# Holding seven half-units of batch 1 instead of six, and re-spacing the reloads of batch 0, in a two-pass kernel bound by its transfers

## The chip, the cores and the metric

The kernel runs on one core of a Trainium2 chip. The metric is the device time of one execution in microseconds. The kernel before took 1709.55 us (median of three runs, 1707.28 to 1709.72).

## The reference, cut to what matters

`x` has the shape (2, 512, 256, 256), f32: 2 batches, 512 channels, 268 MB. The output has the same shape.

```python
xn = group_norm(x)                      # 32 groups of 16 channels, mean and variance per (b, group)
xl1 = relu(batch_norm(depthwise(xn, w1)))   # w1: 256 x 1, contracts the rows    -> (b, c, 256)
xl2 = relu(batch_norm(depthwise(xn, w2)))   # w2: 1 x 256, contracts the columns -> (b, c, 256)
dot = sum(xl1 * xl2, axis=-1)           # (b, c); the einsum's result is read as c x b and reshaped
num = softmax((dot.reshape(b, c) @ lw1.T + lb1) @ lw2.T + lb2, axis=1)
out = x + xn * num[:, :, None, None]    # = x * scale(b, group, channel) + shift(b, group, channel)
```

The einsum `bck,bck->cb` followed by `reshape(b, c)` mixes the batches: row 0 of the softmax needs the dot products of both batches over channels 0 to 255, row 1 those over channels 256 to 511. So the scales of batch 0 are known when half of the channels of both batches have been read, those of batch 1 only when everything has.

## The kernel before

The work is cut into half-units (u, b): u from 0 to 63 is one half of the rows of a group of 16 channels (group g = u // 2), b is the batch. A half-unit is 128 partitions x 4096 f32 = 2048 KB. There are 128 of them; on the chip there are eleven places for one: ten buffers of `xs` (0 to 9) and `filters` (number 10, called FILTERS).

The pass reads every half-unit once for its statistics. Per half-unit ACT squares it (L805), PE convolves it with w1 (L576, in the last three groups L591, one batch at a time), and DVE multiplies the rows with w2 and sums them (16 row instructions at L1002, or one product and one reduction over the whole half-unit at L1028 and L1031, or sums of products that POOL made). Scaling and storing comes later, and what has left its buffer by then has to be loaded again:

- Batch 0, units 0 to 31: the first four scaled are still in their buffers (KEPT = 4), the other 28 are loaded again ("reloads" 0 to 27, `load_again`, L331) during the second half of the pass. ACT scales each (L878) and stores it (L883) in `rework(r)`.
- Batch 0, units 32 to 63: scaled in their buffers as soon as the group's statistics are there (`scale_first` on DVE, L1104; `store_first` on ACT).
- Batch 1: all 64 are scaled after the pass. The last HELD ones are still in their buffers, the others are loaded again (L378), scaled by DVE (L1174) and stored by ACT in the order LAST_ORDER, round the eleven places of `last_slot`. This last stretch is called the tail.

All orders are written out by hand. SP issues every load in one fixed order and waits before each until the buffer is free, so a load that waits holds up all loads behind it. ACT issues nearly all stores, in its program order. In the second half of the pass a step is a pair (g, b): SP issues the two loads of it, then the reload whose number REWORK_AT assigns to step 2g + b. ACT does that reload's scaling in the same step. `rework_slot(r)` gives a reload its buffer (2, 3 and 8 in turn for most), `slot_of(u, b)` gives a half-unit of the pass its buffer: batch 1 takes 6 and 7 in turn, except those held to the end.

`softmax(1)` at the end of the pass (L1166) is a chain through all engines: the last row sums on DVE, `normalise(15)`, `rectify(15)` and `exponential(1)` on ACT (L863, L869, L874), the logits on PE, the coefficients on DVE. Only then may the first half-unit of batch 1 be scaled and stored.

Line numbers are those of the kernel before; everything below the edit is five to seven lines further down in the changed one.

Of the kernel before, what the change touches and what calls it, by code (L numbers as in the profile page):

```python
# [11 lines left out]
UNITS = 2 * G  # L12
S = 11
SCRATCH, FILTERS = 9, 10
# [17 lines left out]
FIRST = UNITS // 2  # L32
# [1 line left out]
FQ = Q // 2  # L34
RING3 = 27
KEPT = 4
HELD = 6
REWORK = FIRST - KEPT
PROD_SLOT = SCRATCH
PROD_GROUPS = range(FG + 2, G - 4)  # L40
CHUNKS = 2
CHUNK_ROWS = JH // CHUNKS
REWORK_AT = list(range(FIRST + 1, UNITS - 6)) + [UNITS - 5, UNITS - 3]
ACT_SCALES = G - 3
SPLIT = G - 3
LAST_ORDER = list(range(UNITS - HELD, UNITS)) + list(range(UNITS - HELD))
# [17 lines left out]
def slot_of(u, b):  # L64
    if u < RING3:
        return u % 3 + 4 * b
    if u < FIRST:
        return u % 4 + 4 * b
    if b == 0:
        return (4, 5, 0, 1)[u % 4]  # L70
    return {UNITS - 6: 9, UNITS - 5: 2, UNITS - 2: 4, UNITS - 1: 5}.get(u, 6 + u % 2)


def rework_slot(r):
    if r < 2:
        return (8, PROD_SLOT)[r]
    if r < REWORK - 4:
        return (2, 3, 8)[(r - 2) % 3]
    return (3, 8, 3, 8)[r - REWORK + 4]


def last_slot(i):
    return (9, 2, 6, 7, 4, 5, 3, 8, 0, 1, FILTERS)[i % S]


LOADS = [[] for _ in range(S)]
# [26 lines left out]
def conv_preact(nc, x, w1, w2, g1, b1, g2, b2, w2_rows, lw1, lb1, lw2, lb2, out):  # L113
# [9 lines left out]
    with ExitStack() as ctx:  # L123
# [172 lines left out]
        @block.sync  # L296
        def _(sp):
            def free_of_statistics(u, b):
                sp.wait_ge(rows_done, rows_before(u, b) + SETS)
                sp.wait_ge(squared, position(u, b) + 1)  # L300
                if u < FIRST:
                    sp.wait_ge(multiplied, position(u, b) + 1)
                sp.wait_ge(pe_read_x, filters_before(u, b))

            def load(u, b):
                s = slot_of(u, b)
                n = LOADS[s].index(("x", u, b))
                if n == 0 and s in (3, 7):
                    sp.wait_ge(mixed_copied, CT)
                    sp.wait_ge(bias_copied, 1)  # L310
                elif n:
                    before = LOADS[s][n - 1]
                    if before in STORES[s]:
                        sp.wait_ge(x_stored[s], written(s, before))
                        if s == PROD_SLOT:
                            sp.wait_ge(rows_done, rows_before(2 * PROD_GROUPS[-1] + 1, 0) + SETS)
                    else:
                        free_of_statistics(before[1], before[2])
                sp.dma_start(xs[:, s, :], x_v[u // 2, :, b, part_of(u)]).then_inc(x_loaded[s], 16)

            def load_again(r):
                s = rework_slot(r)
                n = LOADS[s].index(("re", r))
                if s == SCRATCH and n == 0:
                    sp.wait_ge(y2_done, FIRST)
                if n:
                    before = LOADS[s][n - 1]
                    if before[0] == "x":
                        before = ("x", FIRST - KEPT + s, 0)
                    sp.wait_ge(x_stored[s], written(s, before))  # L330
                sp.dma_start(xs[:, s, :], x_v[r // 2, :, 0, part_of(r)]).then_inc(x_loaded[s], 16)  # L331

            sp.dma_start(w2_c[:], w2_rows.rearrange("(t p) w -> p t w", p=P)).then_inc(w2c_loaded, 16)
            load(0, 0)
            sp.dma_start(w1_sb[:], w1).then_inc(w1_loaded, 16)
            load(0, 1)
            load(1, 0)
            load(1, 1)
            sp.dma_start(w2_sb, w2).then_inc(w2_loaded, 16)
            for i, v in enumerate((g1, b1, g2, b2)):  # L340
                sp.dma_start(affine_in[:, i], v.unsqueeze(0).to_broadcast([GB, CG, G])).then_inc(small_loaded, 16)
            sp.dma_start(lb1_sb[:], lb1).then_inc(small_loaded, 16)
            sp.dma_start(bias[:], lb2).then_inc(small_loaded, 16)
            load(2, 0)
            load(2, 1)
            sp.wait_ge(taps_summed, 1)
            sp.dma_start(lw1_sb.rearrange("p (t b) o k -> p t b (o k)", b=B),
                         lw1.rearrange("(t p b) o -> p t b o", p=P, b=B)).then_inc(lw1_loaded, 16)
            sp.dma_start(lw2_sb, lw2.rearrange("(o p) c -> p o c", p=P)).then_inc(lw2_loaded, 16)
            for u in range(3, FIRST):  # L350
                for b in range(B):
                    load(u, b)

            load_again(0)
            for u, b in SEQUENCE[2 * FIRST:2 * FIRST + 4]:
                load(u, b)
            load_again(1)
            for i in range(0, KEPT, 2):
                u = FIRST - KEPT + i
                sp.wait_ge(scaled_kept[0], i // 2 + 1)  # L360
                sp.dma_start(out_v[u // 2, :, 0, part_of(u)], xs[:, slot_of(u, 0), :]
                             ).then_inc(x_stored[slot_of(u, 0)], 16)
            for g in range(FG + 1, G):
                for b in range(B):
                    for hf in range(2):
                        load(2 * g + hf, b)
                    if 2 * g + b in REWORK_AT:
                        load_again(REWORK_AT.index(2 * g + b) + 1)

            for i in range(HELD, UNITS):  # L370
                s, u = last_slot(i), LAST_ORDER[i]
                if i >= S:
                    sp.wait_ge(x_stored[s], written(s, ("last", i - S)))
                elif s == FILTERS:
                    sp.wait_ge(pe_read_x, filters_before(UNITS - 1, 1))
                else:
                    sp.wait_ge(x_stored[s], written(s, LOADS[s][LOADS[s].index(("last", i)) - 1]))
                sp.dma_start(buffer(s), x_v[u // 2, :, 1, part_of(u)]).then_inc(x_loaded[s], 16)  # L378
            for s in range(S):
                sp.wait_ge(x_stored[s], 16 * len(STORES[s]))  # L380
# [418 lines left out]
        def _(act):  # L799
# [52 lines left out]
            def normalise(q):  # L852
                r = rstd_a[:, q, QG * B:] if q < FQ else rstd_b[:, QG * (q + 1) - 1 - FG, B:2 * B]
                act.wait_ge(off_ready, q + 1)
                act.wait_ge(folded, QG * (q + 1))
                act.wait_ge(y2_turned, q + 1)
                if q:
                    act.wait_ge(dots_ready, 2 * q)
                if q == FQ:
                    act.wait_ge(prob_turned, 1)  # L860
                for i, (to, y) in enumerate(((z, ps_y1), (ps_y2, ps_y2))):
                    for b in range(B):
                        nc.scalar.activation(to[:, b * W:(b + 1) * W], y[:, b * W:(b + 1) * W], ACT.Identity,  # L863
                                             scale=r[:, b:b + 1], bias=off[:, i, b:b + 1]).then_inc(z_done, 1)

            def rectify(q):
                act.wait_ge(affine_ready, q + 1)
                for i, y in enumerate((z, ps_y2)):
                    nc.scalar.activation(y[:], y[:], ACT.Relu, scale=bn_a[:, i:i + 1],  # L869
                                         bias=bn_b[:, i:i + 1]).then_inc(relu_done, 1)  # L870
# [14 lines left out]
            def rework(r):  # L885
                s = rework_slot(r)
                act.wait_ge(x_loaded[s], landed(s, ("re", r)))
                scaled_by_act(s, r // 2, reworked, r + 1)
                store(r, 0, s)
# [35 lines left out]
            for i in range(1, KEPT, 2):  # L925
                u = FIRST - KEPT + i
# [4 lines left out]
            for u, b in SEQUENCE[2 * FIRST:]:  # L931
                if u % 2 == 0 and b == 0 and u // 2 in PROD_GROUPS:
                    copy_w2_late(u // 2)
                square(u, b)
                if u % 2:
                    if u // 2 >= SPLIT:
                        copy_part(u // 2, b)
                    elif b:
                        copy_parts(u // 2)
                        store_first(u // 2)  # L940
                    if u - 1 + b in REWORK_AT:
                        rework(REWORK_AT.index(u - 1 + b) + 1)
                elif b and u // 2 >= SPLIT:
                    store_first(u // 2)
                for q in range(FQ, Q - 1):
                    if position(u, b) == stage(q, 23):
                        normalise(q)
                    if position(u, b) == stage(q, 27):
                        rectify(q)
            normalise(Q - 1)  # L950
            rectify(Q - 1)
            exponential(1)
# [254 lines left out]
```

## Time and profile before

| | |
|---|---|
| median of 3 runs | 1709.55 us |
| the profiled execution | 1705.58 us, its span 1703.8 us |
| busy | DVE 1004.7 us (59%), ACT 665.1 (39%), POOL 508.9 (30%), PE 485.6 (28%) |
| DMA | 723.80 MB at a mean of 425 GB/s |
| first store of batch 1 after the pass | issued at 1128.04 us |

The profile was taken in one execution. "DMA share" is the mean busy share of the core's 16 DMA engines; a share of 1.00 or 1.01 means that they had work all the time. The DMA queue q1 carries the loads, which SP issues, and q10 the stores, which ACT issues. A transfer's time to landing counts from its issue, so it includes the time that it stood behind others in its queue. Microseconds in the rows count from the start of the span.

### The profile page before, as it was taken

The page shows a single profiled execution, that of the slowest core. Times are in us where ns is not written, and L with a number is a line of the kernel's source. Part 1 is how long each engine was busy: PE and PEld are TensorE (multiplying, and loading weights), DVE is VectorE, ACT ScalarE, POOL GpSimd, SP SyncE. Part 2 cuts the span into 40 slices and gives each one's busy share as a digit, 9 for nine tenths or more (in the row PEclk, how much of TensorE's full clock was granted, in tenths as well). Part 3 has the DMA queues.
Part 4 walks back from the last instruction along what each step waited for, and adds up shares of the span by engine and source line. Part 5 has one row for each costly group of instructions (what it writes and reads, how often), then busy time and mean ns, then how long its engine had stood idle before and what let it go on. Part 6 is the DMA issues. An engine that isn't in the chain of part 4 may idle for free.

```text
span 1703.8 us, 14430 instructions
## 1 busy us (share of the span) xinstructions
PE 485.6 (28%) x3416; PEld 169.7 (10%) x3416; DVE 1004.7 (59%) x2672; ACT 665.1 (39%) x517; POOL 508.9 (30%) x489
## 2 busy tenths in 40 slices
PE   3588766660223321223333243430000000000000
PEld 1123212120001100001001021210000000000000
DVE  5899999967757576776666786772222222222220
ACT  4688887856435455544445546600000000000000
POOL 7678787820315444443254000000000000000000
PEclk8799878885666665666566566665555555555555
DMA  9999999989999999999999999999999999999999
GB/s 393 426 425 427 427 428 426 428 338 419 432 428 431 431 430 431 430 432 430 432 430 430 431 428 430 430 385 431 431 432 431 432 431 431 432 431 432 431 431 408
DMA packets 52126, 723.80 MB, mean 425 GB/s; under 512 B 6241, under 2 KB 6753, under 8 KB 8034
## 3 DMA queue, kind: packets, MB, share of 16 engines
q1 hardware_dynamic: 33922, 458.84, 63.4%
q10 hardware_dynamic: 18144, 264.25, 36.3%
q8 instruction: 27, 0.44, 0.1%
q14 instruction: 33, 0.27, 0.0%
HBM read 454.63 MB, written 268.44 MB: 424 GB/s over the span
## 4 chain that ended last, share of the span: by engine, by line
DMA 39%; another core or an unknown queue 26%; DVE 8%; PE 3%; issue 2%; ACT 2%; SPq 1%; DVEq 1%; POOL 0%; ACTq 0%; POOLq 0%
DMA xs<-in_x 28%; DMA out<-xs 11%; DVE xs L1104 3%; PE ps_part L576 2%; DVE xs L1028 1%; DVE mul_junk L1002 1%; DVE y2s L1031 1%; SPq L378 1%; ACT xs L878 1%; PE ps_part L710 1%; ACT sq_junk L805 1%; DVEq L1002 0%; DVE xs L1002 0%; POOL rstd_b L468 0%
## 5 line engine op out<-in xcount | busy, mean ns | idle before, releaser
L805 ACT ACTIVATE sq_junk<-xs 128x4096 fp8e5<-128x4096 f32 x128 | 463.1, 3618 | 203.9 <-DMA xs<-in_x 198.6
L576 PE MATMUL ps_part<-xs,filters 128*32 128x512 f32 x1856 | 290.8, 781 | 525.3 <-DMA xs<-in_x 516.2
L1104 DVE TENSOR_SCALAR xs<-xs,scale,shift 128x4096 f32<-128x4096 f32 x90 | 222.8, 2496 | 353.9 <-DMA xs<-in_x 353.3
L1002 DVE SCALAR_TENSOR_TENSOR xs<-xs,ps_w 128x256 f32 (+1 forms) x832 | 294.5, 416 | 28.6 <-DMA xs<-in_x 18.4
L534 POOL TENSOR_TENSOR xs<-xs,w_late 128x2048 f32<-128x2048 f32 x40 | 179.6, 4526 | 102.6 <-ACT w_late L819 102.6
L878 ACT ACTIVATE xs<-xs,shift,scale 128x4096 f32<-128x4096 f32 x33 | 125.3, 3798 | 157.3 <-DVE xs L1104 135.5
L576 PEld LDWEIGHTS ps_part<-xs,filters 128*32 128x32 f32 x1856 | 79.3, 138 | 718.3 <-issue 718.3
L1028 DVE TENSOR_TENSOR xs<-xs,ps_w 128x4096 f32<-128x4096 f32 x26 | 114.7, 4413 | 52.8 <-PE ps_part L576 46.6
L468 POOL TENSOR_TENSOR rstd_b<-var,minus_half 128x2 f32<-128x2 f32 (+1 forms) x23 | 15.2, 661 | 417.2 <-DVE var L1054 417.2
L1022 DVE TENSOR_REDUCE y2s<-xs 128x8 f32<-128x2048 f32 x40 | 91.4, 2286 | 77.1 <-POOL xs L534 77.1
L439 POOL TENSOR_TENSOR xs<-xs 128x768 f32<-128x768 f32 x64 | 116.7, 1827 | 58.0 <-DMA xs<-in_x 55.0
L1002 DVE SCALAR_TENSOR_TENSOR mul_junk<-xs,ps_w 128x256 uint8<-128x256 f32 x288 | 104.1, 417 | 30.5 <-DVE mul_junk L1002 15.9
L1031 DVE TENSOR_REDUCE y2s<-xs 128x16 f32<-128x4096 f32 x26 | 114.9, 4420 | 2.7
L1002 DVE DVE_READ_ACCUMULATOR xs<-xs,ps_w (+1 forms) x832 | 68.3, 82 | 0.0
L445 POOL TENSOR_TENSOR xs<-xs 128x384 f32<-128x384 f32 x64 | 63.1, 1009 | 0.0
L591 PE MATMUL ps_part<-xs,filters 128*32 128x256 f32 x384 | 38.6, 566 | 52.8 <-DMA xs<-in_x 52.8
L449 POOL TENSOR_TENSOR xs<-xs 128x192 f32<-128x192 f32 x64 | 36.8, 600 | 0.0
L409 POOL TENSOR_TENSOR filters<-own,filters 128x512 f32<-128x512 f32 x32 | 33.9, 1059 | 6.9 <-PE ps_part L591 6.7
L604 PE MATMUL ps_y<-y_part,fold 128*32 128x512 f32 x64 | 31.0, 615 | 4.5 <-ACT y_part L833 4.4
L826 ACT ACTIVATE y_part<-ps_part 128x256 f32<-128x256 f32 x58 | 21.6, 382 | 26.4 <-PE ps_part L576 17.8
L672 PE MATMUL ps_l<-xs 128*128 128x512 f32 x64 | 29.6, 605 | 0.0
L1104 DVE TENSOR_SCALAR filters<-filters,scale,shift 128x4096 f32<-128x4096 f32 x5 | 12.1, 2410 | 29.2 <-DMA filters<-in_x 29.2
(116 smaller groups left out, 458.4 us busy)
## 6 DMA issues: line engine op xcount, KB each, us to landing
xs<-in_x SPq DMA_DIRECT2D x209, 2048.0 KB, 24.0
out<-xs ACTq DMA_DIRECT2D x121, 2048.0 KB, 27.6
filters<-in_x SPq DMA_DIRECT2D x5, 2048.0 KB, 18.0
out<-filters ACTq DMA_DIRECT2D x5, 2048.0 KB, 86.2
xs<-in_lw SPq DMA_DIRECT2D x2, 2048.0 KB, 16.3
out<-xs SPq DMA_DIRECT2D x2, 2048.0 KB, 12.1
filters<-in_w_rows SPq DMA_DIRECT2D x1, 512.0 KB, 3.8
filters<-in_w SPq DMA_DIRECT2D x1, 512.0 KB, 8.9
```

The source lines that it names most:

```text
L439: nc.gpsimd.tensor_tensor(prod[:, b], xs[:, s, DVE_ROWS * W:].rearrange("p (r w) -> p r w", w=W), w2_copy[:, g % 2].unsqueeze(1).to_broadc ...
L445: nc.gpsimd.tensor_tensor(prod[:, b, :, 0:128], prod[:, b, :, 0:128], prod[:, b, :, 128:256], ALU.add).then_inc(added, 1)
L534: nc.gpsimd.tensor_tensor(chunk(c), x_rows[:, c * CHUNK_ROWS:(c + 1) * CHUNK_ROWS], w2_late[:].unsqueeze(1).to_broadcast([P, CHUNK_ROWS, W ...
L576: last = nc.tensor.matmul(ps_part[g % 2][32 * a:32 * a + 32, :], taps[:, g % 2, hf * JH + j, :], xs[:, s[0]:s[1] + 1:s[1] - s[0], j * W:(j ...
L591: last = nc.tensor.matmul(ps_part[b][32 * a:32 * a + 32, 0:W], taps[:, g % 2, hf * JH + j, :], xs[:, s, j * W:(j + 1) * W], start=(hf == 0 ...
L805: nc.scalar.activation(sq_junk[:], xs[:, s, :], ACT.Square, accum_out=sq_sum[:, u % 2, u // 2, b:b + 1], saturate=False).then_inc(squared, 1)
L878: nc.scalar.activation(xs[:, s, :], xs[:, s, :], ACT.Identity, scale=scale[:, 0, g:g + 1], bias=shift[:, 0, g:g + 1]).then_inc(done, 1)
L1002: return nc.vector.scalar_tensor_tensor(out=out, in0=x_row, scalar=1.0, in1=ps_w2[g % 2][:, 0:W], op0=ALU.mult, op1=ALU.mult, accum_out=total)
L1022: nc.vector.tensor_reduce(sums[:, c * CHUNK_ROWS:(c + 1) * CHUNK_ROWS], chunk(c), AX.X, ALU.add).then_inc(rows_done, SETS // CHUNKS)
L1028: nc.vector.tensor_tensor(x_rows, x_rows, ps_w2[g % 2][:, 0:W].unsqueeze(1).to_broadcast([P, JH, W]), ALU.mult).then_inc(products_done, 1)
L1031: nc.vector.tensor_reduce(sums, x_rows, AX.X, ALU.add).then_inc(rows_done, SETS)
L1104: return nc.vector.tensor_scalar(buffer(s), buffer(s), scale[:, b, g:g + 1], shift[:, b, g:g + 1], ALU.mult, ALU.add)
```

## The change

One more half-unit of batch 1, (57, 1), stays in its buffer at the end of the pass (HELD = 7, in buffer 8), so the tail has 57 loads in place of 58. The reloads of batch 0 move: three steps in the middle of the second half of the pass (38, 43 and 48) issue two reloads each; behind step 54 only step 57 has one; the last reload (27) is issued behind all loads of the pass, and ACT scales and stores it behind the last half-unit and ahead of `normalise(15)`. The tail goes round its places in another order. Since (57, 1) is now held, DVE treats it with 16 row instructions, as it did the six.

```diff
@@ -34,13 +34,14 @@
 FQ = Q // 2
 RING3 = 27
 KEPT = 4
-HELD = 6
+HELD = 7
 REWORK = FIRST - KEPT
 PROD_SLOT = SCRATCH
 PROD_GROUPS = range(FG + 2, G - 4)
 CHUNKS = 2
 CHUNK_ROWS = JH // CHUNKS
-REWORK_AT = list(range(FIRST + 1, UNITS - 6)) + [UNITS - 5, UNITS - 3]
+TWICE = (FIRST + 6, FIRST + 11, FIRST + 16)
+REWORK_AT = sorted([*range(FIRST + 1, UNITS - 9), *TWICE, UNITS - 7])
 ACT_SCALES = G - 3
 SPLIT = G - 3
 LAST_ORDER = list(range(UNITS - HELD, UNITS)) + list(range(UNITS - HELD))
@@ -68,19 +69,23 @@
         return u % 4 + 4 * b
     if b == 0:
         return (4, 5, 0, 1)[u % 4]
-    return {UNITS - 6: 9, UNITS - 5: 2, UNITS - 2: 4, UNITS - 1: 5}.get(u, 6 + u % 2)
+    return {UNITS - 7: 8, UNITS - 6: 9, UNITS - 5: 2, UNITS - 2: 4, UNITS - 1: 5}.get(u, 6 + u % 2)
 
 
 def rework_slot(r):
     if r < 2:
         return (8, PROD_SLOT)[r]
-    if r < REWORK - 4:
+    if r < REWORK - 2:
         return (2, 3, 8)[(r - 2) % 3]
-    return (3, 8, 3, 8)[r - REWORK + 4]
+    return 3
+
+
+def reworks_at(step):
+    return [r for r, at in enumerate(REWORK_AT, 1) if at == step]
 
 
 def last_slot(i):
-    return (9, 2, 6, 7, 4, 5, 3, 8, 0, 1, FILTERS)[i % S]
+    return (8, 9, 2, 6, 7, 4, 5, FILTERS, 0, 1, 3)[i % S]
 
 
 LOADS = [[] for _ in range(S)]
@@ -364,8 +369,9 @@
                 for b in range(B):
                     for hf in range(2):
                         load(2 * g + hf, b)
-                    if 2 * g + b in REWORK_AT:
-                        load_again(REWORK_AT.index(2 * g + b) + 1)
+                    for r in reworks_at(2 * g + b):
+                        load_again(r)
+            load_again(REWORK - 1)
 
             for i in range(HELD, UNITS):
                 s, u = last_slot(i), LAST_ORDER[i]
@@ -938,8 +944,8 @@
                     elif b:
                         copy_parts(u // 2)
                         store_first(u // 2)
-                    if u - 1 + b in REWORK_AT:
-                        rework(REWORK_AT.index(u - 1 + b) + 1)
+                    for r in reworks_at(u - 1 + b):
+                        rework(r)
                 elif b and u // 2 >= SPLIT:
                     store_first(u // 2)
                 for q in range(FQ, Q - 1):
@@ -947,6 +953,7 @@
                         normalise(q)
                     if position(u, b) == stage(q, 27):
                         rectify(q)
+            rework(REWORK - 1)
             normalise(Q - 1)
             rectify(Q - 1)
             exponential(1)
```

On SP, around step 43 (both rows of loads of group 21 batch 1, its reload, then group 22), the kernel before has this order; x_stored2 means that the transfer waits until what stood in buffer 2 has been stored:

```order
L319 DMA xs<-in_x 128x4096 [waits pe_read_x,squared,rows_done] x2
L331 DMA xs<-in_x 128x4096 [waits x_stored2]
L319 DMA xs<-in_x 128x4096 [waits x_stored4]
L319 DMA xs<-in_x 128x4096 [waits x_stored5]
L331 DMA xs<-in_x 128x4096 [waits x_stored3]
L319 DMA xs<-in_x 128x4096 [waits pe_read_x,squared,rows_done] x2
L331 DMA xs<-in_x 128x4096 [waits x_stored8]
```

The same place in the changed kernel:

```order
L324 DMA xs<-in_x 128x4096 [waits pe_read_x,squared,rows_done] x2
L336 DMA xs<-in_x 128x4096 [waits x_stored3]
L336 DMA xs<-in_x 128x4096 [waits x_stored8]
L324 DMA xs<-in_x 128x4096 [waits x_stored4]
L324 DMA xs<-in_x 128x4096 [waits x_stored5]
L336 DMA xs<-in_x 128x4096 [waits x_stored2]
L324 DMA xs<-in_x 128x4096 [waits pe_read_x,squared,rows_done] x2
```

Two reloads (12 and 13, buffers 3 and 8) now stand ahead of the loads of group 22; the second waits for the store of a reload two steps back, where every reload before waited for one three steps back.

On SP, from (54, 0) to (59, 1), before. The two rows with x2 are (54, 1), (55, 1) and (56, 1), (57, 1):

```order
L319 DMA xs<-in_x 128x4096 [waits x_stored1]
L331 DMA xs<-in_x 128x4096 [waits x_stored8]
L319 DMA xs<-in_x 128x4096 [waits pe_read_x,squared,rows_done] x2
L331 DMA xs<-in_x 128x4096 [waits x_stored2]
L319 DMA xs<-in_x 128x4096 [waits x_stored4]
L319 DMA xs<-in_x 128x4096 [waits x_stored5]
L331 DMA xs<-in_x 128x4096 [waits x_stored3]
L319 DMA xs<-in_x 128x4096 [waits pe_read_x,squared,rows_done] x2
L331 DMA xs<-in_x 128x4096 [waits x_stored8]
L319 DMA xs<-in_x 128x4096 [waits x_stored0]
L319 DMA xs<-in_x 128x4096 [waits x_stored1]
```

The same half-units in the changed kernel:

```order
L324 DMA xs<-in_x 128x4096 [waits x_stored1]
L336 DMA xs<-in_x 128x4096 [waits x_stored8]
L324 DMA xs<-in_x 128x4096 [waits pe_read_x,squared,rows_done] x2
L324 DMA xs<-in_x 128x4096 [waits x_stored4]
L324 DMA xs<-in_x 128x4096 [waits x_stored5]
L324 DMA xs<-in_x 128x4096 [waits pe_read_x,squared,rows_done]
L324 DMA xs<-in_x 128x4096 [waits x_stored8]
L336 DMA xs<-in_x 128x4096 [waits x_stored3]
L324 DMA xs<-in_x 128x4096 [waits x_stored0]
L324 DMA xs<-in_x 128x4096 [waits x_stored1]
```

The reloads before are 22, 23, 24 and 25; now they are 25 and 26. The load of (57, 1) goes to buffer 8 and waits for the store of reload 25.

On SP, from (60, 1) to the first loads of the tail, before:

```order
L319 DMA xs<-in_x 128x4096 [waits pe_read_x,squared,rows_done] x2
L331 DMA xs<-in_x 128x4096 [waits x_stored8]
L319 DMA xs<-in_x 128x4096 [waits x_stored0]
L319 DMA xs<-in_x 128x4096 [waits x_stored1]
L319 DMA xs<-in_x 128x4096 [waits x_stored4]
L319 DMA xs<-in_x 128x4096 [waits x_stored5]
L378 DMA xs<-in_x 128x4096 [waits x_stored3]
L378 DMA xs<-in_x 128x4096 [waits x_stored8]
L378 DMA xs<-in_x 128x4096 [waits x_stored0]
L378 DMA xs<-in_x 128x4096 [waits x_stored1]
L378 DMA filters<-in_x 128x4096 [waits pe_read_x]
L378 DMA xs<-in_x 128x4096 [waits x_stored9]
```

The same place in the changed kernel:

```order
L324 DMA xs<-in_x 128x4096 [waits pe_read_x,squared,rows_done] x2
L324 DMA xs<-in_x 128x4096 [waits x_stored0]
L324 DMA xs<-in_x 128x4096 [waits x_stored1]
L324 DMA xs<-in_x 128x4096 [waits x_stored4]
L324 DMA xs<-in_x 128x4096 [waits x_stored5]
L336 DMA xs<-in_x 128x4096 [waits x_stored3]
L384 DMA filters<-in_x 128x4096 [waits pe_read_x]
L384 DMA xs<-in_x 128x4096 [waits x_stored0]
L384 DMA xs<-in_x 128x4096 [waits x_stored1]
L384 DMA xs<-in_x 128x4096 [waits x_stored3]
L384 DMA xs<-in_x 128x4096 [waits x_stored8]
```

Reload 27 moved from ahead of (62, 0) to behind (63, 1). Before, five loads of the tail came ahead of the first that waits for a store of batch 1 (x_stored9); now four do, and `filters` is the first of them in place of the last.

## Rows read from the trace of the kernel before

**Rows 1.** The profile's page: span, DMA busy tenths and GB/s in 40 slices.
```profile
span 1703.8 us, 14430 instructions
...
DMA  9999999989999999999999999999999999999999
GB/s 393 426 425 427 427 428 426 428 338 419 432 428 431 431 430 431 430 432 430 432 430 430 431 428 430 430 385 431 431 432 431 432 431 431 432 431 432 431 431 408
```
**Rows 2.** Stretches: us, PE, PEld, DVE, ACT, POOL busy, clock, DMA share, GB/s.
```profile
600.00:800.00 200.00, 55.95 (x390) 17.73 (x390) 139.60 (x75) 101.09 (x67) 83.02 (x38) 0.64 1.01 431
...
950.00:1104.00 154.00, 66.15 (x566) 28.75 (x566) 115.23 (x471) 89.45 (x58) 8.12 (x19) 0.62 1.01 430
```
**Rows 3.** The same view, the end of the pass and the tail.
```profile
1104.00:1136.00 32.00, 15.63 (x120) 7.92 (x120) 20.05 (x55) 5.21 (x12) 3.28 (x10) 0.67 0.93 374
1112.00:1124.00 12.00, 9.14 (x22) 3.60 (x22) 3.24 (x10) 4.02 (x8) 1.88 (x7) 0.74 0.79 315
1136.00:1680.00 544.00, 0.00 (x0) 0.00 (x0) 143.06 (x60) 0.00 (x0) 0.00 (x0) 0.50 1.01 431
```
**Rows 4.** The page: DMA issues, KB each, median us to landing.
```profile
xs<-in_x SPq DMA_DIRECT2D x209, 2048.0 KB, 24.0
out<-xs ACTq DMA_DIRECT2D x121, 2048.0 KB, 27.6
filters<-in_x SPq DMA_DIRECT2D x5, 2048.0 KB, 18.0
out<-filters ACTq DMA_DIRECT2D x5, 2048.0 KB, 86.2
...
out<-xs SPq DMA_DIRECT2D x2, 2048.0 KB, 12.1
```
**Rows 5.** Timeline of SP's queue at the end of the pass: start us, us.
```profile
1120.51 0.43 SPq L378 DMA_DIRECT2D filters<-in_x  x1
```
**Rows 6.** That transfer by its line: us from issue to landing.
```profile
DMA to landing us min/median/max: 13.4/13.4/13.4
```
**Rows 7.** Timeline of SP's queue around (57, 1).
```profile
954.83 19.75 SPq L319 DMA_DIRECT2D xs<-in_x  x4
984.08 0.33 SPq L331 DMA_DIRECT2D xs<-in_x  x1
```
**Rows 8.** Timeline of PE: the convolution of (57, 1); brackets: idle before, released by.
```profile
975.57 4.96 PE L576 MATMUL ps_part<-xs,filters 128*32 128x512 f32 x32 [3.38 <-DMA xs<-in_x]
```
**Rows 9.** Timeline of ACT at the end of the pass.
```profile
1101.01 3.62 ACT L805 ACTIVATE sq_junk<-xs 128x4096 fp8e5<-128x4096 f32 x1 [0.47 <-ACT xs L878]
...
1111.89 0.56 ACT L863 ACTIVATE z<-ps_y,off,rstd_b 128x256 f32<-128x256 f32 x1 [6.81 <-PE ps_y L616]
```
**Rows 10.** Timeline of ACT's queue: the stores of the tail begin.
```profile
1128.04 21.24 ACTq L883 DMA_DIRECT2D out<-xs  x10
```
**Rows 11.** Waits of DVE, 1035 to 1095 us: us in total, times, longest.
```profile
DVE mul_junk L1002 <- DMA xs<-in_x: 13.8, 4, 6.9
```
**Rows 12.** Timeline of DVE: (57, 1), then (62, 0) and what follows it.
```profile
990.12 4.41 DVE L1028 TENSOR_TENSOR xs<-xs,ps_w 128x4096 f32<-128x4096 f32 x1
994.63 4.42 DVE L1031 TENSOR_REDUCE y2s<-xs 128x16 f32<-128x4096 f32 x1
...
1075.49 0.42 DVE L1002 SCALAR_TENSOR_TENSOR mul_junk<-xs,ps_w 128x256 uint8<-128x256 f32 x1 [3.90 <-DMA xs<-in_x]
...
1081.97 0.15 DVE L1048 TENSOR_SCALAR nmean<-ps_m 128x1 f32<-128x1 f32 x1
```
**Rows 13.** The page: ACT scales a reload; busy us, mean ns | idle before.
```profile
L878 ACT ACTIVATE xs<-xs,shift,scale 128x4096 f32<-128x4096 f32 x33 | 125.3, 3798 | 157.3 <-DVE xs L1104 135.5
```
**Rows 14.** Timeline of SP's queue: the reloads of steps 45 and 46.
```profile
657.34 0.47 SPq L331 DMA_DIRECT2D xs<-in_x  x1
...
678.82 0.33 SPq L331 DMA_DIRECT2D xs<-in_x  x1
```
**Rows 15.** Loads of line L319 issued from 600 to 700 us.
```profile
DMA to landing us min/median/max: 23.8/32.0/36.5
```

## The prediction, made before the changed kernel had run

> **What bounds the kernel now.** I read the page's slices of DMA first, then stretches of the same counters, and only then single engines. The DMA engines are busy at nine tenths or more in all slices but one, and they move 426 to 432 GB/s in most of them [rows 1]. Two slices of the 40 stand out: 338 in slice 9 and 385 in slice 27 [rows 1]. The change touches only the second. In the second half of the pass and in the tail the DMA share is 1.00 or 1.01 at 430 to 431 GB/s [rows 2, 3], while DVE, the busiest engine, has 140 us of 200 [rows 2]. So the time is the bytes, at 430 GB/s, and the places where the transfers run dry. One transfer of 2048 KB (2.097 MB) costs 2.097 / 430 = 4.88 us. There are 342 of them (209 + 5 loads, 121 + 5 + 2 stores [rows 4]), which is 1669 us of the span of 1704.
>
> The dry place is the end of the pass. From 1104 to 1136 us the rate is 374 in place of 430: 32 x (1 - 374/430) = 4.2 us are lost [rows 3]; 3.2 of them lie in 1112 to 1124, at 315 GB/s [rows 3]. There the chain of `softmax(1)` runs, no half-unit of batch 1 may be stored before 1128.04 [rows 10], and the reloads that could fill the time wait in SP's queue: the one into `filters` was issued at 1120.51 [rows 5] and landed 13.4 us later [rows 6], behind two that waited for the stores of (62, 0) and (63, 0), though PE had long left `filters`.
>
> **The sum is made against the profiled execution**, 1705.6 us (span 1703.8). The median of the runs is 1709.55, 4.0 us more; I take the difference worked out here to the median.
>
> **One reload less.** The tail has 57 loads in place of 58: -4.9 us. Nothing covers a transfer where the share is 1.01 for 544 us [rows 3], so this is on the path in full.
>
> **The dry place.** To be moved between the last load of the pass and the first store of batch 1 were five tail loads, the store of reload 27 and two stores; now four tail loads, reload 27 with its load and store, and the two stores: one transfer more of cover. `filters` comes first and waits only for PE, so it can flow while the stores of (62, 0) and (63, 0) are under way. How much of the 4.2 us comes back depends on when compute releases the first store of batch 1 against when the DMA has moved all that stands ahead of it. The second time: before, the `filters` load landed at 1133.9; from 1128.0 it shared the engines with stores, so half of these 5.9 us, 2.9, was its own. 1128.0 + 2.9 - 4.2 (dry) - 4.9 (the reload less) = 1121.8 us. Every us that the first store comes after 1121.8 is lost.
>
> **When compute is ready.** The anchor is (57, 1): PE starts to convolve it at 975.57, released by its load [rows 8]. From there to the first store of batch 1 are 1128.04 - 975.57 = 152.5 us. In these DVE waited four times for loads of the pass, 13.8 us in all [rows 11]; with three reloads fewer between (57, 1) and (63, 1) these waits go. DVE also works less: (57, 1) took 4.4 + 4.4 us as product and reduction, 16 row instructions take 1081.97 - 1075.49 = 6.5 [rows 12]: -2.3. So the floor is 152.5 - 13.8 - 2.3 = 136.4 us behind the landing of (57, 1). Any faster pass ends on DVE, no longer on the loads.
>
> That landing comes later, since reloads have moved ahead of it. Counted in transfers: before, reloads 0 to 24 were loaded ahead of (57, 1), and the stores of 0 to 23 had landed (the fourth of SP's loads from 954.83, which needs store 23, leaves at 974.3; reload 26, which needs store 24, at 984.08 [rows 7]). Now 0 to 25 are loaded ahead of it and the stores of 0 to 25 have landed, because its buffer waits for store 25. That is one load and two stores: 3 x 4.88 = 14.6 us. The load is issued earlier than before, so a part of the stores of (54, 0) and (55, 0) may fall behind it: 0 to 9.8 us off. I take half a transfer: +12.2, so 987.8. The first store then comes at 987.8 + 136.4 = 1124.2, and the loss is 1124.2 - 1121.8 = 2.4 us in place of 4.2: -1.8. The bounds: landing 4.9 us later gives 1116.9 and no loss, -4.2; 14.6 later gives 1126.6, a loss of 4.8, +0.6.
>
> A sentence of the Trainium skill speaks against this term: DMA: Bandwidth & Descriptors, "Anatomy of one DMA", gives each transfer a fixed cost of about 2.0 us (fitted for transfers that GpSimd issues), which shows wherever nothing else is under way; the three tail loads that wait for a store each would show it again, so by that page nothing of the 4.2 us comes back and the sum would be the 4.9 of the reload alone. No row here shows the cost by itself. The mechanism by rows: each of these loads is issued only when a store has landed, and 3.2 us were lost with two such loads [rows 3, 5]; now `filters` and reload 27 lie beside them. It is the first rival below.
>
> **Reload 27 ahead of normalise(15) on ACT.** ACT gets its last square at 1101.01, which ends with the copy behind it by 1105.1, and `normalise(15)` starts at 1111.89, released by PE [rows 9]. Scaling a reload takes 3.8 us [rows 13], its issue 0.3: 1109.2, 2.7 us before it is needed. If the reload lands over 2.7 us after ACT is free, the softmax chain and the first store slip by the rest. It follows (63, 1) at once in its queue, 4.9 to 9.8 us behind it (alone, or taking turns with stores), and (63, 1) now comes earlier against DVE. I take 0; the bound is +4.1 (9.8 - 3.0 for the square - 2.7).
>
> **The double steps.** The second reload of a double step waits for a store two steps back. At the same point before, SP passed a reload at 657.34, and the store from two steps back had landed at 678.82 [rows 14]: SP, and with it the loads of the next group, would stand for 21.5 us. In its queue lie then loads issued 23.8 to 36.5 us ahead of their landing [rows 15], one more than before, and the stores. So the DMA does not run dry: 0. Engines wait longer for half-units, which costs nothing while the share is 1.01. If another 9.8 us of waiting for the next reload's store came on top, 31.3 against 23.8 + 4.9 would leave 2.6 us dry, three times: +8.
>
> **Sum:** -4.9 - 1.8 + 0 + 0 = -6.7 us, -0.39%: 1698.9 in the profiled execution, 1702.8 on the median. Its own range, from the bounds of the landing, is -9.1 to -4.3: 1700.4 to 1705.3.
>
> **Rivals.**
> 1. Only the reload is saved; the dry place keeps its 4.2 us since the loads at its end still depend on stores, or ACT's reload delays the chain. -4.9: 1704.7. For it: the loads into buffers 0, 1 and 3 all wait for late stores. Against: one transfer more in the stretch.
> 2. Nothing: the double steps run dry. 1709.55 - 6.7 + 8 = 1710.9, or half of it, 1707. For it: SP's block of 21.5 us is as long as the shortest queue of 23.8. Against: the share of 1.01 through stretches in which SP waits as it is [rows 2]; a deep queue.
> 3. Slower: (57, 1) comes so late that the rest of the pass is bound by DVE. If all three advanced reloads with loads and stores fall ahead of it (6 x 4.88 = 29.3), it lands at 1004.9, the first store of batch 1 is issued at 1141.3, 19.5 us behind 1121.8, and the sum is -4.9 - 4.2 + 19.5 = +10.4: 1719.9. It decides from a loss of 9.1 us on, that is from a landing 18.9 us later than before, four transfers against my three. For it: DVE, once behind, has no slack in 136 us. Against: two of the six transfers come behind (57, 1) by the order itself.
>
> **How the numbers follow.** The forecast 0.50, rival 1 0.22, rival 2 0.17, rival 3 0.11. A measurement of this kernel tells a change from about 0.2% on, 3.4 us; so faster by more is 0.50 + 0.22 = 0.72, within it 0.17, slower 0.11. The predicted time is 1702.8. The range that leaves two in ten out is 1699.5 (the low bound of the forecast and a little for the spread of the runs) to 1709.5 (rival 1 and half of rival 2).
>
> **What would show it.** Right: 341 transfers; DMA share 1.01 in 430 to 1100 us as before; PE's convolution of (57, 1) at 980 to 990; DVE without waits for DMA from (60, 0) on; over 400 GB/s in the 12 us ahead of a first store of batch 1 at 1117 to 1127; ACT's reload 27 done before PE releases `normalise(15)`. Wrong: slices below 425 GB/s between 450 and 950 us (rival 2); that convolution behind 994 and a wide dry stretch ahead of the first store (rival 3); the same 4 us dry and a first store near 1128 (rival 1).

## The result: 0.3% slower, where 0.4% faster was forecast

The changed kernel takes 1712.65 us (median of 9 runs, 1710.7 to 1715.8), the kernel before, beside it, 1708.35 (9 runs). The ratio is 1.0031, 95% interval 1.0022 to 1.0040: 4 to 5 us slower (3.8 to 6.8 by the interval). The forecast was 1702.8, its range 1699.5 to 1709.5. The profiled execution of the changed kernel took 1712.33 us, its span 1710.6, 6.8 us more than before [rows 1].

### The profile after

The page of the changed kernel has the reload less (213 loads against 214), and slices 23 to 27 where the rate falls, where before only slice 27 did [rows 1, 4]:

```profile
span 1710.6 us, 14489 instructions
...
GB/s 394 425 427 427 427 427 426 428 354 417 433 429 432 431 429 432 430 429 432 429 432 431 414 416 395 348 415 427 429 428 431 431 430 433 430 431 433 430 431 402
...
xs<-in_x SPq DMA_DIRECT2D x207, 2048.0 KB, 22.2
...
filters<-in_x SPq DMA_DIRECT2D x6, 2048.0 KB, 18.2
```

Stretches of the changed kernel, with the columns of [rows 2]:

```profile
430.00:950.00 520.00, 137.72 (x946) 44.46 (x950) 332.41 (x175) 256.64 (x167) 204.22 (x91) 0.63 1.01 431
950.00:1050.00 100.00, 45.00 (x386) 18.51 (x382) 84.53 (x251) 47.16 (x37) 9.15 (x14) 0.68 1.00 412
1050.00:1110.00 60.00, 28.36 (x266) 13.73 (x258) 51.00 (x260) 35.49 (x25) 4.41 (x13) 0.73 0.88 354
1110.00:1140.00 30.00, 16.22 (x120) 8.06 (x120) 17.36 (x57) 9.90 (x13) 3.26 (x10) 0.61 1.00 418
1140.00:1680.00 540.00, 0.00 (x0) 0.00 (x0) 146.59 (x62) 0.00 (x0) 0.00 (x0) 0.50 1.01 430
```

The same in the kernel before, for the three in the middle:

```profile
950.00:1050.00 100.00, 39.00 (x344) 16.48 (x344) 74.28 (x267) 53.28 (x35) 5.92 (x13) 0.59 1.01 430
1050.00:1110.00 60.00, 31.48 (x274) 14.85 (x270) 46.09 (x237) 37.24 (x27) 2.20 (x6) 0.67 1.01 430
1110.00:1140.00 30.00, 11.29 (x88) 5.34 (x80) 18.91 (x27) 4.13 (x8) 3.28 (x10) 0.67 0.92 368
```

Against 430 GB/s, before lost 30 x 62/430 = 4.3 us, all in the last stretch. The changed kernel loses 100 x 18/430 = 4.2, 60 x 76/430 = 10.6 and 30 x 12/430 = 0.8, together 15.6. The dry place was cured as forecast (368 to 418), and a larger one opened inside the pass. 15.6 - 4.3 - 4.9 (the reload) = +6.4, of the 6.8 measured between the two spans. That this comes so near is partly luck: in e11, a second profile of the same kernel, the same three stretches lose 12.4 us, and the span is 0.6 us longer. What holds in both is the first store of batch 1: it is 7.6 us later than before (1135.63 against 1128.04), and from it to the end pass 575.0 us, 575.8 before; 7.6 - 0.8 = 6.8. Up to 950 us, through all three double steps, the rate is 431 as before.

What opened it is seen on DVE. Timelines of the end of (55, 1) and the start of (56, 1), before:

```profile
947.81 4.42 DVE L1031 TENSOR_REDUCE y2s<-xs 128x16 f32<-128x4096 f32 x1
...
972.31 4.42 DVE L1028 TENSOR_TENSOR xs<-xs,ps_w 128x4096 f32<-128x4096 f32 x1 [6.35 <-PE ps_part L576]
```

and in the changed kernel:

```profile
977.56 4.42 DVE L1038 TENSOR_REDUCE y2s<-xs 128x16 f32<-128x4096 f32 x1
...
995.63 4.42 DVE L1035 TENSOR_TENSOR xs<-xs,ps_w 128x4096 f32<-128x4096 f32 x1
```

DVE ends (55, 1) at 982.0 in place of 952.2, 29.8 us later: about the six transfers (29.3) of the three reloads moved ahead. Before, after the row sums of (56, 0) and (57, 0), it waited 6.35 us for (56, 1); now it waits for nothing there. PE's timeline of the changed kernel shows when (55, 1) and (57, 1) had come. Before, their rows started at 926.04 and 975.57 [rows 8]; (55, 1) came 29.9 us later, but (57, 1) only 13.2 us:

```profile
955.90 5.23 PE L582 MATMUL ps_part<-xs,filters 128*32 128x512 f32 x32 [4.74 <-DMA xs<-in_x]
...
988.77 5.34 PE L582 MATMUL ps_part<-xs,filters 128*32 128x512 f32 x32 [4.12 <-DMA xs<-in_x]
```

The waits of DVE from 952 to 1136 us in the changed kernel hold no wait for a load at all, where before there were 13.8 us of them [rows 11]; the longest are within the row sums themselves and for POOL:

```profile
DVE mul_junk L1009 <- DVE mul_junk L1009: 14.6, 53, 0.6
DVE scale L1117 <- POOL nmr_b L475: 6.2, 5, 2.3
```

The end of the pass on ACT, changed kernel: store of (63, 0), square and copy of (63, 1), reload 27, normalise, first store of batch 1:

```profile
1107.58 0.34 ACTq L889 DMA_DIRECT2D out<-xs  x1
1108.02 3.62 ACT L811 ACTIVATE sq_junk<-xs 128x4096 fp8e5<-128x4096 f32 x1 [0.47 <-ACT xs L884]
...
1111.99 3.79 ACT L884 ACTIVATE xs<-xs,shift,scale 128x4096 f32<-128x4096 f32 x1
1115.81 0.34 ACTq L889 DMA_DIRECT2D out<-xs  x1
1118.90 1.02 ACT L869 ACTIVATE z<-ps_y,off,rstd_b 128x256 f32<-128x256 f32 x2 [3.12 <-PE ps_y L622]
...
1135.63 2.66 ACTq L889 DMA_DIRECT2D out<-xs  x2
```

Reload 27 is scaled and its store issued 2.7 us before `normalise(15)` starts, and that start still waits for PE: reload 27 did not delay the chain. The first store of batch 1 is issued at 1135.63, 7.6 us later than before [rows 10].

### The profile page after: what moved, and what is told of

It reads as the page before. It is cut to its first block, busy times and chain, and to the rows that moved or that the text cites. A ratio compares the mean times of both kernels' runs of the same rounds, so it can differ in the third digit from the quotient of the medians.

```text
span 1710.6 us, 14489 instructions
## 1 busy us (share of the span) xinstructions
PE 486.4 (28%) x3416; PEld 172.8 (10%) x3416; DVE 1000.8 (59%) x2702; ACT 664.3 (39%) x517; POOL 508.4 (30%) x489
## 4 chain that ended last, share of the span: by engine, by line
DMA 35%; another core or an unknown queue 25%; DVE 10%; issue 5%; PE 3%; ACT 2%; DVEq 2%; SPq 1%; POOL 0%; ACTq 0%; POOLq 0%
DMA xs<-in_x 22%; DMA out<-xs 13%; DVE mul_junk L1009 3%; DVE xs L1111 3%; ACT xs L884 2%; DVE xs L1035 1%; PE ps_part L582 1%; DVEq L1009 1%; SPq L384 1%; DVE y2s L1038 1%; PE ps_part L716 1%; ACT sq_junk L811 1%; DVE xs L1009 0%; DVEq L1040 0%
## 5 line engine op out<-in xcount | busy, mean ns | idle before, releaser
L1035 DVE TENSOR_TENSOR xs<-xs,ps_w 128x4096 f32<-128x4096 f32 x25 | 110.3, 4413 | 71.5 <-PE ps_part L582 65.4
L1009 DVE SCALAR_TENSOR_TENSOR mul_junk<-xs,ps_w 128x256 uint8<-128x256 f32 x304 | 109.8, 417 | 18.9 <-DVE mul_junk L1009 18.2
L1038 DVE TENSOR_REDUCE y2s<-xs 128x16 f32<-128x4096 f32 x25 | 110.5, 4420 | 2.6
L832 ACT ACTIVATE y_part<-ps_part 128x256 f32<-128x256 f32 x58 | 21.6, 381 | 25.7 <-PE ps_part L582 15.6
```

The lines of the kernel that those rows point to most:

```text
L1009: return nc.vector.scalar_tensor_tensor(out=out, in0=x_row, scalar=1.0, in1=ps_w2[g % 2][:, 0:W], op0=ALU.mult, op1=ALU.mult, accum_out=total)
L1035: nc.vector.tensor_tensor(x_rows, x_rows, ps_w2[g % 2][:, 0:W].unsqueeze(1).to_broadcast([P, JH, W]), ALU.mult).then_inc(products_done, 1)
L1038: nc.vector.tensor_reduce(sums, x_rows, AX.X, ALU.add).then_inc(rows_done, SETS)
```

## The experiments

All ratios are to the kernel before on the same chip, with 95% intervals. The runs were made on several chips, so kernels are compared by their ratios, and medians are set side by side only where a chip is shared or the gap is large. "First store" is the issue of the first store of batch 1 in the one profiled execution of each run. The code excerpts show the lines that matter and leave out the rest of the edit. Theory A: the reloads taken out of steps 55 to 61 had covered DVE's work there. The rivals stand in the expectations.

**e1: reload 27 behind the pass, alone** (against the kernel before)

```diff
-REWORK_AT = list(range(FIRST + 1, UNITS - 6)) + [UNITS - 5, UNITS - 3]
+REWORK_AT = list(range(FIRST + 1, UNITS - 6)) + [UNITS - 5]
-    return (9, 2, 6, 7, 4, 5, 3, 8, 0, 1, FILTERS)[i % S]
+    return (9, 2, 6, 7, 4, 5, 3, FILTERS, 0, 1, 8)[i % S]
```

Not shown: the load of reload 27 behind the pass, into buffer 8, and its scaling ahead of `normalise(15)`, as in the change.

> The kernel before with one part of the change alone: reload 27 is issued behind (63, 1), and ACT scales and stores it ahead of normalise(15); six half-units held, the other reloads where they were. Theory A (the change lost its time because the reloads taken out of steps 55 to 61 had covered the time that DVE needs there; DVE was 14 us late for the first store of batch 1): here DVE is not late at (55, 1), its four waits for loads (13.8 us) go, the first store of batch 1 comes near 1114 to 1118 in place of 1128, and the 4.2 us of the dry place go: 1704 to 1706 against 1708.4. Theory B (reload 27 behind the pass is itself what costs, on ACT ahead of the softmax chain or as a dependent tail load): no faster, or 1 to 4 us slower, with the first store of batch 1 at 1128 or later.

1706.01 us, ratio 0.9990 (0.9981 to 0.9999); first store at 1121.79. Behind the pass, reload 27 does no harm: the first store comes 6 us earlier. But that is 4 us later than A's 1114 to 1118, the time only touches the upper end of A's range, and the gain is 2 us where A expected 4.2, because 1050 to 1110 now runs at 410 GB/s (2.8 us lost). So a thin place opens there even where only reload 27 is taken out of the last groups.

**e2 and e12: the reloads moved ahead, alone** (against the changed kernel; e12 is the same kernel again)

```diff
-HELD = 7
+HELD = 6
-REWORK_AT = sorted([*range(FIRST + 1, UNITS - 9), *TWICE, UNITS - 7])
+REWORK_AT = sorted([*range(FIRST + 1, UNITS - 9), *TWICE, UNITS - 7, UNITS - 3])
```

Not shown: the buffers and the order of the tail go back to those of the kernel before, and reload 27 (step 61) is loaded and scaled inside the pass.

> The kernel before with the reloads moved ahead alone: double steps 38, 43, 48, then only steps 57 and 61; six held, the old buffers and the old tail order. Theory A: DVE ends (55, 1) near 982 in place of 952, the first store of batch 1 comes near 1135 to 1138, DMA is short of work from 1050 to 1110, and the kernel is 5 to 8 us slower than before, 1714 to 1716. Theory B (holding a seventh half-unit, the tail's new order or reload 27 costs): within 1 us of before. Theory C (the double steps cost by themselves, SP standing in front of the second reload): slower too, but with the loss between 480 and 800 us, below 425 GB/s there.

> The kernel of e2 (the reloads moved ahead alone, reload 27 at step 61, six held) beside the changed kernel. In the profiled execution of e2 (1714.4 us) the first store of batch 1 came at 1139.7; its median was 4 us below that execution. Theory A: 1713 to 1717 and slower than the changed kernel. If it stays below the changed kernel, holding the seventh half-unit and moving reload 27 behind the pass together cost 2 us and save nothing in this schedule: what they take from the last groups is lost again on DVE.

e2: 1710.51, ratio 1.0022 (1.0011 to 1.0033), first store at 1139.72 in an execution 3.9 us above the median. e12: 1710.71, 1.0022 (1.0013 to 1.0032), first store at 1136.10. The move alone makes the kernel about 4 us slower, where 5 to 8 were expected, so theory B is out. The rate is 431 in 600 to 950 us in both, so theory C is out.

**e11: the changed kernel again, beside e12**

> The changed kernel itself, on the chip and beside the runs of e12. Theory A puts it at 1712 to 1713 again, and below e12 by the reload less, 3 to 5 us, if both lose the same time at the end of the pass. So far their medians (1712.65 and 1710.51, on other chips) say the opposite.

1712.87, ratio 1.0023 (1.0014 to 1.0031); first store at 1135.81. So the changed kernel is not faster than e12 with its 342 transfers; the intervals overlap. Both start the tail at the same time, and have the same tail before them: 64 stores and 53 loads (57 less the four, 58 less the five that come ahead of it). From the first store to the end of the span pass 1711.2 - 1135.8 = 575.4 and 1709.0 - 1136.1 = 572.9 us; 117 transfers at 4.88 are 571. The two kernels differ by one transfer ahead of the first store, and that store is issued at the same time. So by this count the reload that was saved had lain in time that is now dry. This part is argued from the count; e12's 2.5 us less behind the first store are not explained. Stretches of e12, then two of e11:

```profile
950.00:1050.00 100.00, 43.40 (x386) 17.95 (x382) 87.84 (x221) 47.45 (x37) 7.27 (x14) 0.65 1.00 421
1050.00:1110.00 60.00, 29.20 (x266) 13.78 (x258) 50.96 (x259) 39.46 (x26) 4.41 (x13) 0.73 0.99 408
1110.00:1140.00 30.00, 17.01 (x120) 8.07 (x120) 16.67 (x57) 5.89 (x12) 3.27 (x10) 0.61 0.86 361
...
950.00:1050.00 100.00, 46.52 (x389) 18.63 (x382) 84.86 (x252) 47.40 (x37) 9.31 (x14) 0.67 1.01 429
1050.00:1110.00 60.00, 28.09 (x266) 13.29 (x258) 50.90 (x259) 35.49 (x25) 4.40 (x13) 0.70 0.86 344
```

In e11 950 to 1050 us loses 0.2 us, where the first profile of this kernel lost 4.2; 1050 to 1110 loses 12.0 against 10.6. Only the second place belongs to the change in both.

**e4 and e5: a quarter of DVE's row sums left out in units 56 to 63**, in the changed kernel (e4) and in the kernel before (e5)

```diff
-                    for j in range(SET):
+                    for j in range(SET if u < UNITS - 8 else SET - 1):
```

> The changed kernel with a quarter of DVE's row instructions left out in the 15 half-units of units 56 to 63 that are summed row by row (12 of 16 rows each, the row sums of the others are missing): 60 instructions, some 24 us of DVE, and no transfer changed. Theory A (DVE is what ends last there): the first store of batch 1 comes 14 to 24 us earlier, DMA is no longer short of work from 1064 to 1112, and 9 to 14 us go: 1698.5 to 1704. Theory D (the loads wait for stores whose landing the DMA queues set, DVE is beside the path): 0 to 3 us go, 1710 to 1712.6.

> The kernel before with the same quarter of the row instructions left out in units 56 to 63 (14 half-units, 56 instructions, some 22 us of DVE; their row sums are missing). The other half of the test of e4. Theory A (in the kernel before, DVE waits for loads there and only its last instructions count): the 22 us turn into longer waits for loads; the first store of batch 1 comes 1 to 4 us earlier, 1705 to 1708 against 1708. Theory D (DVE's row work is worth its time in either kernel, so e4 told nothing of the change): 9 us go as in e4, 1699.

e4: 1703.28, ratio 0.9973 (0.9962 to 0.9983); first store at 1120.84. e5: 1707.31, 0.9998 (0.9988 to 1.0007); first store at 1129.78, not the 1 to 4 us earlier that A expected. The same work left out is worth about 9 us in the changed kernel (8.5 to 10 by the ratios) and nothing in the kernel before, where it turns into waits. DVE's waits from 952 to 1112 us in e5, where the kernel before has 13.8 and 6.3 us in the same two groups:

```profile
DVE mul_junk L1002 <- DMA xs<-in_x: 21.0, 4, 9.3
...
DVE xs L1028 <- PE ps_part L576: 12.1, 1, 12.1
```

and the stretch of e4 that was at 354 GB/s:

```profile
1050.00:1110.00 60.00, 30.90 (x317) 15.80 (x318) 40.88 (x198) 38.30 (x28) 6.75 (x20) 0.72 0.97 405
```

This is the pair that shows DVE to be the bound there, and only in the changed kernel; theory D is out. It does not account for everything: e4 still runs at 413 GB/s in 950 to 1050 and at 405 in 1050 to 1110.

**e6: ACT scales four more half-units, in the complete changed kernel**

```diff
-ACT_SCALES = G - 3
+ACT_SCALES = G - 7
```

> The changed kernel, complete, with ACT in place of DVE scaling the second half-unit of batch 0 of groups 25 to 28 too (ACT_SCALES = G - 7): 4 instructions of 2.4 us leave DVE, 4 of 3.8 us come to ACT; no transfer changes. Theory A: DVE, the bound from (55, 1) on, is 5 to 9 us earlier, and so is the first store of batch 1: 1704 to 1708 against 1712.65. Theory D (DVE is beside the path): no gain, or 1 to 3 us lost because each of these four stores leaves 1.4 us later.

1706.81, ratio 0.9994 (0.9984 to 1.0004); first store at 1132.59. 5 to 6 us faster than the changed kernel by its two ratios (1.0023 and 1.0031), by taking 4 instructions of 2.4 us from DVE in the complete kernel. The first store is from an execution 3.1 us above the median.

**e9: the double steps at 49, 51 and 53** (against the changed kernel)

```diff
-TWICE = (FIRST + 6, FIRST + 11, FIRST + 16)
+TWICE = (FIRST + 17, FIRST + 19, FIRST + 21)
```

> The changed kernel with the three double steps at 49, 51 and 53 in place of 38, 43 and 48; everything from step 54 on, and so what is missing there, is the same. Theory A (what counts is that three reloads fewer lie in the last groups): within 2 us of the changed kernel. Theory C (double steps in the middle cost by themselves, by SP standing 20 us in front of the second reload): several us faster, as the damage has less time; or, if the queue of loads is not deep enough for three doubles close together, slower with rates below 425 GB/s between 830 and 950 us.

1712.91, ratio 1.0024 (1.0015 to 1.0033); first store at 1135.96. Where the double steps stand makes no difference that shows; 830 to 950 us runs at 431 GB/s with all three close together. What counts is what is missing behind step 54.

**e3: seven held without double steps** (against the changed kernel)

```diff
-REWORK_AT = sorted([*range(FIRST + 1, UNITS - 9), *TWICE, UNITS - 7])
+REWORK_AT = list(range(FIRST + 1, UNITS - 6)) + [UNITS - 5]
-    return {UNITS - 7: 8, UNITS - 6: 9, UNITS - 5: 2, UNITS - 2: 4, UNITS - 1: 5}.get(u, 6 + u % 2)
+    return {UNITS - 6: 9, UNITS - 5: 2, UNITS - 3: 8, UNITS - 2: 4, UNITS - 1: 5}.get(u, 6 + u % 2)
-    return (8, 9, 2, 6, 7, 4, 5, FILTERS, 0, 1, 3)[i % S]
+    return (7, 9, 2, 6, 8, 4, 5, FILTERS, 0, 1, 3)[i % S]
```

> Seven held as in the change and reload 27 behind the pass, but no double steps: (57, 1) stays in buffer 7 where the kernel before puts it, (61, 1) goes to buffer 8, so reloads 1 to 25 keep their steps, 26 stays at step 59. Theory A: the reload less (-4.9) is kept and the dry place goes (up to -4.2), first store of batch 1 near 1112 to 1120: 1699 to 1703. Theory B (the seventh held or the last reload behind costs): as slow as the changed kernel, or no faster than before, 1708 to 1713.

1703.28, ratio 0.9974 (0.9964 to 0.9985); first store at 1124.15, later than A's 1112 to 1120. With (57, 1) in buffer 7 and (61, 1) in buffer 8, buffer 8 must be free four steps later, and no reload has to move ahead. Beside e1 on the same chip, which differs by the seventh half-unit held and the buffers that go with it, e3 is 2.7 us faster: with DVE not late, holding it pays, but only a part of its 4.9 us, since e3 loses time at 391 GB/s in 1050 to 1110 (5.4 us, e1 2.8).

**e7: e3 with reload 26 at step 61**

```diff
-REWORK_AT = list(range(FIRST + 1, UNITS - 6)) + [UNITS - 5]
+REWORK_AT = list(range(FIRST + 1, UNITS - 6)) + [UNITS - 3]
```

> e3_other_buffer with reload 26 at step 61 in place of 59. In e3 the DMA was short of work at 1062 to 1098 us (321 to 406 GB/s), 5 us lost, since loads waited for stores that waited for DVE. If what is missing there is any transfer that can flow, reload 26 and its store fill it: 1 to 4 us faster than e3's 1703.3. If SP's order counts more (reload 27 waits for the store of reload 26 and holds the tail loads up behind it), nothing or 1 to 3 us slower.

1701.93, ratio 0.9965 (0.9952 to 0.9978); first store at 1119.69. It has the lowest median, 0.35% faster than before, but its interval overlaps e3's, so the gain on e3 is not shown. Its stretches:

```profile
950.00:1050.00 100.00, 44.53 (x406) 19.69 (x410) 80.17 (x323) 56.05 (x39) 6.63 (x15) 0.62 1.01 430
1050.00:1110.00 60.00, 30.67 (x269) 14.97 (x262) 42.25 (x220) 39.53 (x28) 4.73 (x14) 0.66 0.98 408
1110.00:1140.00 30.00, 6.12 (x20) 2.19 (x18) 24.51 (x20) 0.77 (x2) 0.00 (x0) 0.61 1.00 409
```

**e8 and e10: e3 and e7 with ACT scaling more** (ACT_SCALES = G - 7 and G - 5)

> e3_other_buffer with ACT scaling the second half-unit of groups 25 to 28 too. In e3 DVE still waits 12.4 us for loads after 960 us, so by theory A only a part of the 7 to 10 us taken from DVE counts: 0 to 3 us faster than 1703.3. Theory D: no gain or slower by the later stores.

> e7_reload26_later, the fastest so far (1701.9), with ACT scaling the second half-unit of groups 27 and 28 too. In e7 the DMA still loses some 3 us at 1050 to 1110 (408 GB/s). Theory A: 0 to 3 us faster, 1699 to 1702. If these stores leaving 1.4 us later count for as much as DVE's 2.4 us: no change, as in e8 against e3.

e8: 1703.03, ratio 0.9967 (0.9956 to 0.9978). e10: 1702.23, 0.9965 (0.9952 to 0.9978). Neither differs from its base: in e8 the same four instructions that helped by 5 to 6 us where DVE was the bound are worth nothing where it is not (e10 moves two).

## Why the prediction was wrong

- **One reload less, -4.9 us: not a gain by itself.** The load is gone (341 transfers), but it was called on the path in full because nothing covers a transfer in the tail. Four or five tail loads come ahead of the first store of batch 1, and when compute sets that store, a load saved is by the count saved out of dry time (e11 beside e12). In the prediction's own sum the term then cancels: 1121.8 already holds the 4.9, so every us by which the store comes later than 1121.8 takes it back. The formula, given the right first store, holds: 1135.6 - 1121.8 = 13.8 lost, -4.9 - 4.2 + 13.8 = +4.7 us; 4 to 5 were measured in the runs, 6.8 between the two profiled spans.
- **The landing of (57, 1): right.** Forecast at 987.8, PE starts on it at 988.8.
- **When compute is ready: the step that failed.** The floor of 136.4 us was counted from that landing, and 146.9 were measured (1135.63 - 988.77). It took for granted that DVE would be no further behind than in the kernel before, where it still has room to wait for (56, 1) and (57, 1) is taken up 14.6 us after its landing (990.12, [rows 12]). But the reloads moved ahead delay (55, 1) by all six transfers, and (57, 1) by only three. The pass closes up in between. Without reloads a group of the pass is four loads and two stores, 29.3 us by the rate; DVE takes 33.7 us for one (from 982.0 to the end of its last row sum at 1116.6 are four groups, with no wait for a load). So DVE fell 16.6 us further behind the landings (29.8 - 13.2), and had 6.35 of them to spare. Counted from the end of (55, 1), with the waits of the kernel before taken off, the floor comes out: before, 1128.04 - 952.2 = 175.8, less the waits 6.35 and 13.8 and the 2.3 of (57, 1), 153.3; 982.0 + 153.3 = 1135.3, measured 1135.63. This count was made after the result. e4, e5 and e6 show that it is DVE.
- **Rival 3 had the mechanism** (the rest of the pass bound by DVE, the store late, +10.4 at its price), with a chance of 0.11. Its condition, (57, 1) later than 994.5, was never met (988.8): it took the lateness of DVE from the landing of (57, 1), and DVE was late already at (55, 1), which came 29.9 us later.
- **The dry place at the end:** -4.2 back, with up to 2.4 lost again. In the profile 4.3 went to 0.8 there, as forecast; the 2.4 became 13.8 by the formula, 14.8 by the rates (4.2 + 10.6), before 1110 us.
- **Reload 27 on ACT, 0: right** (2.7 us of room forecast, 2.7 between its end and `normalise(15)`). The equal numbers are chance, since both sides of the gap moved.
- **The double steps, 0: right** (431 GB/s to 950 us; e9).
- **The rule on a fixed cost per transfer** (the Trainium skill, DMA: Bandwidth & Descriptors, "Anatomy of one DMA") did not decide. That section of the Trainium skill states the cost for one transfer; how much of it shows beside other transfers was the prediction's own step. In the changed kernel the loads into buffers 0, 1 and 3 stand there as well, and it moved 418 GB/s against 368. The trace does not contradict the size: the shortest time from issue to landing of a tail load in the kernel before is 7.4 us, 2.5 more than the 4.88 by the rate, and may hold time spent beside other transfers.

What stays open: why e7 still loses 3 us in 1050 to 1110, and e1 2.8, with DVE waiting for loads; why 950 to 1050 loses 4 us in some profiles (the changed kernel's first, e4, e9) and none in e11. A better split was not tried beyond e10.

## What to carry to other kernels

Work that only moves bytes is also the cover under which a compute engine catches up. Before moving it out of a stretch, compare the engine's time per step with that of the transfers that remain there: here 33.7 us of DVE for a group against 29.3. A floor for a chain is counted from the last point at which the engine of the chain was waiting for data, not from the landing of a later input. And a transfer saved shortens a kernel bound by its bytes only if the engine that releases the next transfers is not late.

## What was not expected of the hardware

In the first profile of the changed kernel there is a stretch, 968 to 980 us, in which the DMA share is full and the rate is not; between 1064 and 1076 both fall:

```profile
968.00:980.00 12.00, 0.95 (x8) 0.36 (x12) 11.90 (x4) 6.31 (x3) 0.65 (x1) 0.56 1.00 388
1064.00:1076.00 12.00, 2.81 (x30) 1.04 (x22) 9.84 (x46) 4.24 (x2) 0.73 (x2) 0.78 0.72 302
```

Of the 4.2 us lost in 950 to 1050 us at most 1 is seen in the share (1.00 against 1.01). The share alone would have hidden it; the rate has to be read with it. In e11, the same kernel again, 968 to 980 runs at 432 GB/s and 1064 to 1076 at 300, so the first is not a property of the kernel, and the second is. The cause of the first was not looked for.
